# Third layer of a mixture FFN: activations stationary and weights moving 256 wide, in place of weights stationary and activations moving 512 wide

## What is computed

```python
# x: (b, f, 256) after the attention layer, normalised rows; w: (f, 8) softmax gate of the node f
h = relu(_bn(einsum('bfd,edh->bfeh', x, W1) + b1, g1, be1, m1, v1))
h = relu(_bn(einsum('bfeh,ehk->bfek', h, W2) + b2, g2, be2, m2, v2))
y = einsum('bfeh,ehd->bfed', h, Wo) + bo
return x + einsum('bfed,fe->bfd', y, w)
```

## Time and profile before

| | |
|---|---|
| time, median of 3 runs (lowest to highest) | 3055.14 us (3052.9 to 3057.78) |
| span of the profiled execution, first to last instruction | 3053.3 us |
| of the profiled execution, a time beside the span | none is given; the span is the time used for it |
| PE busy | 2929.1 us, 96% |
| PEld busy | 2449.3 us, 80% |
| DVE busy | 1946.5 us, 64% |
| ACT busy | 1701.8 us, 56% |
| POOL busy | 819.0 us, 27% |
| matmuls, and as many weight loads | 14806 |
| mean granted clock of TensorE | 0.981 |

### The profile page before, as it was taken

How to read it: one execution, slowest core, us unless ns; L and a number is a source line. 1 busy time by engine, 2 the same in 40 slices (tenths; PEclk the granted TensorE clock), 3 DMA queues, 4 the chain that set the end, 5 groups by cost and what they waited for, 6 DMA issues and landing times.

```text
span 3053.3 us, 42543 instructions
## 1 busy us (share of the span) xinstructions
PE 2929.1 (96%) x14806; PEld 2449.3 (80%) x14806; DVE 1946.5 (64%) x2843; ACT 1701.8 (56%) x2620; POOL 819.0 (27%) x894
## 2 busy tenths in 40 slices
PE   7898988889899999999999999999999999999998
PEld 7787878878788888888888888888888888888887
DVE  7788878787655556655555555555555555555654
ACT  7787877777654444445444444444444444444444
POOL 5888878788710000000000000000000000010000
PEclk9999999999899999999999999999999999999999
DMA  4343434343310000000000000000000000000000
GB/s 152 126 137 122 137 127 137 122 142 116 105 56 15 21 21 14 14 14 14 14 14 14 14 27 14 14 14 14 14 14 14 14 27 14 14 14 14 14 14 14
DMA packets 86038, 145.60 MB, mean 48 GB/s; under 512 B 7745, under 2 KB 63465, under 8 KB 86001
## 3 DMA queue, kind: packets, MB, share of 16 engines
q1 hardware_dynamic: 86000, 145.13, 14.4%
HBM read 111.52 MB, written 33.59 MB: 48 GB/s over the span
## 4 chain that ended last, share of the span: by engine, by line
PE 73%; DVE 0%; ACT 0%; issue 0%
PE z_ps L52 16%; PE z_ps L54 16%; PE z_ps L53 16%; PE y_ps L54 8%; PE y_ps L53 8%; PE y_ps L52 8%; PE turn_ps L927 1%; PE turn_ps L937 1%; PE y_ps L1012 0%; PE y_ps L961 0%; PE turn_ps L961 0%; ACT h L1044 0%; DVE h_lo L1142 0%; DVE h L1136 0%; DVE xT_lo L1112 0%; DVE ffn_x L1149 0%
## 5 line engine op out<-in xcount | busy, mean ns | idle before, releaser
L1044 ACT ACTIVATE h<-z_ps,bn_shift,bn_scale 128x512 f32<-128x512 f32 x1024 | 741.9, 775 | 1077.4 <-PE z_ps L54 1075.9
L1123 DVE TENSOR_TENSOR h_lo<-h,h_hi 128x1024 fp32r<-128x1024 f32 x256 | 322.8, 1261 | 762.8 <-ACT h_hi L1061 762.8
L86 POOL TENSOR_TENSOR ffn_vareps<-ffn_mv,ln_eps 128x4 f32<-128x4 f32 x32 | 6.5, 203 | 1879.0 <-DVE ffn_mv L80 1879.0
L52 PE MATMUL z_ps<-h_hi,w_hi 128*128 128x512 f32 x1024 | 410.1, 400 | 0.0
L54 PE MATMUL y_ps<-h_hi,wo_lo 128*128 128x512 f32 x1024 | 407.5, 398 | 0.0
L52 PE MATMUL z_ps<-xT_hi,w_hi 128*128 128x512 f32 x1024 | 405.7, 396 | 0.1
L53 PE MATMUL z_ps<-xT_lo,w_hi 128*128 128x512 f32 x1024 | 405.4, 396 | 0.0
L54 PE MATMUL z_ps<-h_hi,w_lo 128*128 128x512 f32 x1024 | 405.4, 396 | 0.0
L53 PE MATMUL y_ps<-h_lo,wo_hi 128*128 128x512 f32 x1024 | 405.2, 396 | 0.0
L54 PE MATMUL z_ps<-xT_hi,w_lo 128*128 128x512 f32 x1024 | 405.2, 396 | 0.0
L53 PE MATMUL z_ps<-h_lo,w_hi 128*128 128x512 f32 x1024 | 404.6, 395 | 0.0
(11 more groups left out here) (128 smaller groups left out, 4990.3 us busy)
## 6 DMA issues: line engine op xcount, KB each, us to landing
adj_sb<-in_adj SPq DMA_DIRECT2D x128, 512.0 KB, 3.4
x_sb<-in_x SPq DMA_DIRECT2D x64, 256.0 KB, 2.8
x_scratch<-x_sb SPq DMA_DIRECT2D x128, 128.0 KB, 1.8
ffn_x<-x_scratch SPq DMA_DIRECT2D x32, 512.0 KB, 3.3
out<-ffn_x SPq DMA_DIRECT2D x32, 512.0 KB, 2.9
w_stage<-in_L_ffn_W SPq DMA_DIRECT2D x16, 256.0 KB, 4.0
w_bc<-w_scratch SPq DMA_DIRECT2D x8, 512.0 KB, 7.5
w_bc<-in_L_ffn_Wo SPq DMA_DIRECT2D x4, 512.0 KB, 5.8
```

The source lines that it names most:

```text
L52: pe.matmul(out, w_hi, x_hi, start=first, stop=False)
L86: pool.tensor_tensor(self.vareps[:, :], self.mv[:, :, 1], self.ln_eps[:, :], ALU.add) \
L1044: return act.activation(dst[:, m, :], src[:, m, :], ACT.Relu, bias=bn_shift[layer][:, col], scale=bn_scale[layer][:, col])
L1123: dve.tensor_tensor(h1_lo[i][:, :, :], h1[:, :, :], bits(h1_hi[i][:, :, :]), ALU.subtract) \
```

## The change

Layer 3 is made by a new function, `layer_rows`. The stationary operand is now a 128x128 block of the activations (`h2_hi` or `h2_lo`, 128 rows of the tile), and the moving operand is 128 x 256 of the weights (`wo_hi` or `wo_lo`). The result lands in `y_ps` with rows on the partitions, 256 features for each of the 4 groups of 128 rows. A step's third layer is then 4 row groups x 2 halves of the contraction x 3 products = 24 matmuls of 256 columns, each with its weight load, in place of 12 of 512 columns. The multiply-adds are the same.

`transpose_y` and ACT's copy into `yT_sb` are gone; DVE adds the residual rows straight from `y_ps`. That addition now stands at the head of DVE's list for slots 7 and 15, and waits for `step_done` of the tile's last step. Layer 3 of the next tile's first expert waits for `out_ready` in place of `yT_ready`. `transpose_x` waits for the low part of the previous tile's input (`xT_lo_ready`), in place of `out_ready`. `wT_sb` gets a buffer of its own.

```diff
-        yT_sb = sb("yT_sb", [P, KB, BANK])
-
-        wT_sb = yT_sb[0:E, :, :].rearrange("e c n -> e (c n)")
+        wT_sb = sb("wT_sb", [E, TB * P])
...
             def transpose_x(n):
 
                 pe.wait_ge(norm.xn_ready, n)
-                wait(pe, S["out_ready"], n - 2)
+                wait(pe, S["xT_lo_ready"], n - 1)
...
-            def transpose_y(n):
-
-                pe.wait_ge(S["yT_ready"], n)
-                for s in range(CT):
-                    for d in range(KB):
-                        at = (s % 2) * D + d * P
-                        last = pe.transpose(turn_ps[:, s // 2, at:at + P], yT_sb[:, d, s * P:(s + 1) * P], ident[:, :])
-                last.then_inc(S["out_psum"], 1)
-
...
+            def layer_rows(e, x_hi, x_lo):
+
+                for s in range(CT):
+                    rows, acc = slice(s * P, (s + 1) * P), y_ps[:, s // 2, (s % 2) * D:(s % 2 + 1) * D]
+                    for k in range(KB):
+                        cols = slice(k * D, (k + 1) * D)
+                        opens = e == 0 and k == 0 and s % 2 == 0
+                        pe.matmul(acc, x_hi[:, k, rows], wo_hi[:, e, cols], start=opens, stop=False,
+                                  skip_group_check=True)
+                        pe.matmul(acc, x_hi[:, k, rows], wo_lo[:, e, cols], start=False, stop=False,
+                                  skip_group_check=True)
+                        done = pe.matmul(acc, x_lo[:, k, rows], wo_hi[:, e, cols], start=False,
+                                         stop=e == E - 1 and k == KB - 1, skip_group_check=True)
+                return done
...
-                if u >= 0 and u % E == E - 1:
-                    transpose_y(b * CH + (u // E + 1))
...
                     if e == 0:
-                        wait(pe, S["yT_ready"], b * CH + (u + 1) // E)
-                    layer(y_ps, wo_hi[:, e, :], wo_lo[:, e, :], h2_hi[n_par(u + 1)], h2_lo[n_par(u + 1)],
-                          e == 0, e == E - 1).then_inc(S["step_done"], 1)
+                        wait(pe, S["out_ready"], b * CH + (u + 1) // E)
+                    layer_rows(e, h2_hi[n_par(u + 1)], h2_lo[n_par(u + 1)]).then_inc(S["step_done"], 1)
...
             def slot(b, u, last):
-                if u >= 0 and u % E == E - 1:
-
-                    act.wait_ge(S["step_done"], b * US + (u + 1))
-                    act.activation(yT_sb[:, :, :], y_ps[:, :, :], ACT.Copy).then_inc(S["yT_ready"], 1)
...
                 tile_ok, tc, tn = next_tile(b, u, last)
+                if u >= 0 and u % E == E - 1:
+                    t = u // E
+                    dve.wait_ge(S["step_done"], b * US + (u + 1))
+                    dve.wait_ge(S["residual_ready"], b * CH + (t + 1))
+                    rows = x1_sb[t][:, :, :].rearrange("p s d -> p (s d)")
+                    dve.tensor_tensor(rows, y_ps[:, :, :].rearrange("p k c -> p (k c)"), rows, ALU.add) \
+                        .then_inc(S["out_ready"], 1)
...
-                if u >= 0 and u % E == E - 1:
-                    t = u // E
-                    dve.wait_ge(S["out_psum"], b * CH + (t + 1))
-                    dve.wait_ge(S["residual_ready"], b * CH + (t + 1))
-                    rows = x1_sb[t][:, :, :].rearrange("p s d -> p (s d)")
-                    dve.tensor_tensor(rows, turn_ps[:, :, :].rearrange("p k c -> p (k c)"), rows, ALU.add) \
-                        .then_inc(S["out_ready"], 1)
```

More of the change, by code:

```diff
@@ L840, in ffn_block @@
             z1_ready h1_ready h1_hi_ready h1_lo_ready z2_ready relu2_ready gated_ready h2_hi_ready h2_lo_ready
-            step_done yT_ready out_psum out_ready
+            step_done out_ready
             featT_psum featT_ready logits_psum logits_ready top_ready centred_ready exp_ready total_ready
@@ L878, in _ @@
             sp.wait_ge(S["wT_ready"], 1)
-            sp.dma_start(w_dram.rearrange("e c n -> e (c n)"), wT_sb).then_inc(w_stored, DMA)
+            sp.dma_start(w_dram.rearrange("e c n -> e (c n)"), wT_sb[:, :]).then_inc(w_stored, DMA)
             sp.wait_ge(w_stored, DMA)
@@ L1031, in copy_gate @@
                 act.wait_ge(S["wT_psum"], 1)
-                act.activation(wT_sb, y_ps[0:E, :, :].rearrange("e k c -> e (k c)"), ACT.Copy) \
+                act.activation(wT_sb[:, :], y_ps[0:E, :, :].rearrange("e k c -> e (k c)"), ACT.Copy) \
                     .then_inc(S["wT_ready"], 1)
```

## The result

The changed kernel takes 3061.2 us (median of 20 runs, 3057.33 to 3065.62), the kernel before 3054.35 us in runs taken with it (20 runs). The ratio is 1.0021, with a 95% interval from 1.0014 to 1.0028: slower by 0.2%, where 3043.5 us and a range up to 3060 were forecast. The profiled execution has a span of 3058.2 us, 4.9 us more than before.

The account below looks back on a forecast made before the run. The PE's instruction list was taken to bound nearly all of the FFN block. Transposes -26.7, third layers +17.3 and tail -2.2 sum to -11.6 us, from 3055.1 to 3043.5 us; range 3035 to 3060.

Parts of the forecast that it names:

- rival C: PE's FFN loop: larger body no longer stays on the core, a fetch each turn, 30 us, 3074 us; chance 5%.
- likeliest case: Whole kernel: the sum of the terms with its small unknowns, 3043.5 us, own range 3037 to 3049; chance 70%.
- the tail: Kernel's end: DVE's addition starts where ACT's copy did, 2.2 us less; clock moves it -1.5 to +0.6 us.
- The transposes: FFN block on the PE: removing `transpose_y` saves 0.86 us for each of 31 groups, 26.7 us less.
- DVE straight behind the last matmul: Kernel's end: DVE's addition follows the last matmul without copy and transposes between, 2.2 us less.
- The third layer: FFN steps on the PE: 24 matmuls at 0.1195 us, 2.868 in place of 2.800 us, 17.3 us more over 255.
- No new wait: PE's third layer of the next tile's first expert: DVE's addition ends with 2.3 us to spare, so no wait.
- rival D: Start of each new tile: DVE's addition is late and the PE waits, about 3055 to 3070 us; chance 2%.
- Rivals A and B: Third layer's matmul price: A, part of 20 ns fixed, 3087 us, 7% (slower); B, little fixed, 3036 or less, 7%.

Follow-up runs that it names:

- b_noturn: Kernel before without the result's transposes and copy, third layer still 512 wide, output not turned back; 3025.88 us (ratio 0.9906).
- b_halves: Kernel before with each 512-column third-layer matmul cut into two of 256, old orientation, loop placed on 7 blocks by 120 idle waits; 3069.03 us (1.0043).
- a_pad44: Changed kernel with 88 idle waits, about 44 instructions, at the end of the PE's attention list, so the loop body starts later; 3033.82 us.
- a_pad100: Changed kernel with 200 idle waits, about 100 instructions, at the end of the PE's attention list; 3035.56 us (ratio 0.9931).
- a_unroll: Changed kernel with the PE's loop over the batch entries written out, so no branch turns back; 3035.32 us (ratio 0.9932).
- b_fat_pad84: Kernel before with 44 idle waits in each PE loop slot and 168 more ahead of the loop, body over 7 blocks; 3055.12 us (1.0002).

## Why the prediction was wrong

**The step that failed is that the loop's code would stay on the core**, rival C, to which I gave 5%. I compared the number of matmuls and loads in the body, 1568, with the room that the Trainium skill gives TensorE ("Runtime: NRT & Kernel Launch", Instruction fetch mechanics: 2048 instructions, in blocks of 256) and said that it fits. Code is kept by whole blocks, and what the body touches of its first and last block counts in full: 1608 instructions from 228 on touch 8 blocks. The runs show that 7 are kept and 8 are not. The 2048 of the Trainium skill are 8 blocks, so one fewer is of use to a loop here. The nine fetches in a run of the body that touches eight blocks fit a room of eight in which the block fetched ahead takes one; no run moves that alone. The sentence of the Trainium skill on a taken branch, in the same section, speaks of a window of only two pages, outside of which the branch waits for a fetch. The wait agrees with the branch of 3.5 us, the window doesn't with the old body, which lies over 6 blocks and turned back in 0.21 us. Part of the warning was in the trace of before: from the numbers of the instructions at its fetches the position could have been worked out ahead, and with it that the new body fills all 8 blocks. That only 7 are of use was in no row.

The price was right: 2 us for each of 15 turns were put into C, worked out of landings of 1.8 us and an unknown share hidden, and that it came out this close is in part luck; 2.10 for each of 14 are measured in the changed kernel, 29.4 us in all, and 1.77 to 3.04 in the others with 8 blocks. With the likeliest case's other terms, C was to give 3074 us; the changed kernel is 13 us below that, for the reasons that follow.

Against the 3043.5 us of the forecast, the turns are +29.4 us, the shorter steps -10 and the tail -1.4: 18 us, and 17.7 are measured.

**The transposes**, -26.7 us, and DVE straight behind the last matmul, -2.2: right. b_noturn, forecast at 3026 with these two terms, took 3025.9.

**The third layer** was mis-sized, on the good side. The forecast was +0.068 us a step. b_halves shows that this is the right price for a 256-column matmul in the old orientation (2.87 us). In the new one it is +0.049, and the two wide layers are 0.02 us shorter in both kernels. So a step costs 5.58 + 2.85 = 8.43 us in place of 8.40, and a tile 68.27 where I forecast 68.60; over 31 tiles that is 10 us. Why the wide layers' starts come closer beside narrow ones, and why the orientation saves 0.02 us, stays open. The Trainium skill's formula ("TensorE: Matmul & The Clock Gate", Back-to-back issue gap) gives 109.2 ns for 256 columns. The Trainium skill has it for an isolated matmul, which the prediction left out; this stream, with a weight load for each matmul, has 118.7.

**No new wait** (rival D): right. The list of waits has none of the PE for DVE's addition, which kept its duration; the only idle time before it is that of the tail:

```profile
L1119 DVE TENSOR_TENSOR ffn_x<-y_ps,ffn_x 128x1024 f32<-128x1024 f32 x32 | 39.0, 1218 | 3.2 <-PE y_ps L949 3.2
```

**The tail** gave 1.4 us more than its term, by the clock: the last third layer took 3.16 us in place of 4.52, inside the bounds given. Which clock the last layer meets differs from run to run (a_pad44, a_pad100 and a_unroll have the lower level in it), so this part is luck.

**Rivals A and B** fall: a narrow matmul has 12 ns over its columns, the wide one 20.

Without the turns, the table of the spans would leave -24.4 us. a_pad44, with the code kept, has a span of 3032.4, which is 20.9 us less than before: the same -19.4 us for its 30 tiles, and the rest, +1.2 at the start and -2.7 at the end, lies in the start of the block, which scatters by some 3 us between the kernels without my saying why, and in the clock in the last third layer. It took 3033.82 us (ratio 0.993, 0.9913 to 0.9948). Both a_pad44 and a_unroll beat both kernels: the change as such is a gain of 0.7%.

## What to carry to other kernels

Before a loop's body on the PE grows, count its instructions (two for each matmul, and the waits) and where it begins and ends in blocks of 256. Here seven blocks were kept, eight were not, and then every turn cost 1.8 to 3.0 us that the profile shows only as "issue" before the body's first matmul. The number of instruction fetches on the page, beside that of before, tells it at a glance; moving the body, or writing the loop out, is the remedy. A net gain that is the small difference of two well-priced terms should be put against every overhead that the larger code may bring, before it is given a high chance.

## What the runs showed of the hardware

- A branch back to code no longer held took 3.3 to 4.4 us against 0.21, over the five kernels with 8 blocks; the longest pause between two starts of matmuls at a turn was then 1.6 to 2.8 us, where 0.24 us is the usual distance of wide ones. Fetching straight on, 16 KB for every 256 instructions, cost nothing in a_unroll's 110 fetches.
- Idle waits were hidden as long as the PE was the bound: 22 instructions of them a slot added nothing measurable in b_fat_pad84 (ratio 1.0002, 0.9992 to 1.0012).
- The granted clock fell for 3.4 us behind two of the 14 turns of the changed kernel, and in none of a_pad44's loop. The window behind one of them (length, busy us, then the clock):

```profile
1961.20:1964.60 3.40, 3.40 (x8) 2.72 (x9) 0.00 (x0) 0.00 (x0) 0.00 (x0) 0.50 0.04 13
```

That is the lower level, 1.2 GHz. The tiles that hold these stretches took 72.01 and 71.85 us where others with a turn took 69.9 to 70.6, so a turn with such a stretch behind it cost nearly as much again.
